# Attention projection: the parts of q and k stored once, and stacks put together by the loads

## The chip, the cores and the metric

One NeuronCore of a Trainium2 chip runs the whole program in one launch. Its engines are TensorE (PE, with its weight loads as PEld), VectorE (DVE), ScalarE (ACT), GpSimd (POOL) and SyncE (SP); 16 DMA engines move data, on one queue that SyncE issues to and one that ScalarE issues to. The metric is the device time of one execution in microseconds. Three executions of the kernel before took 5768.95, 5780.09 and 5784.97 us, the median is 5780.09 us.

## The reference, cut to what matters

The program is a stack of sixteen layers on four sequences of 1024 tokens with 128 features. Five of the layers are attention (layers 2, 4, 6, 8 and 14 of the program). The others (state space layers, ternary and gated feed-forward layers, a mixture of experts) are not touched. An attention layer computes, with 16 heads of 8 features (layer 14: 4 features for q and k):

```
h = layernorm(x)
q, k, v = h @ Wq + bq, h @ Wk + bk, h @ Wv + bv      # split into 16 heads
q, k = rope(q), rope(k)                              # layers 4 and 6 alone
s = q k^T * scale, causal                            # layer 14 adds a slope times the distance
y = softmax(s) v                                     # layer 2 weighs the probabilities by a decay table
x = x + y @ Wo + bo
```

## The kernel before

The residual stream `x` stays in SBUF, features on partitions and 4096 tokens along them. Every layer is a chain of stages; a stage ends when all its engines have reached its end (a barrier), and the next then starts. `attention` (from line 419) has a layer norm, the projection `attn_project` and the core `attn_core`.

**The projection.** The 4096 tokens are worked through in four batches (the sequences), each as two halves of 512 tokens, q and k in turn: four units a batch. TensorE multiplies (L526), VectorE brings the value to SBUF, with a bias or with rotary embedding (L550 to L577), ScalarE rounds it to bf16 (L607, the high part), GpSimd subtracts (L643), ScalarE rounds the rest (L613, the middle part), and the low part is what is then left (L561 on VectorE, or L650 on GpSimd where there is rotary embedding). `part` holds the three bf16 parts of q and k. V is projected last (L532, L595, L598).

**Slots.** Scores are made with bf16 products whose sum comes close to a float32 product: six pairs of a part of q and a part of k, the list `PAIRS`. A head thus needs 6 x 8 rows of q (high, high, high, middle, middle, low) against 6 x 8 rows of k (high, middle, low, high, middle, high). The projection writes all six slots to DRAM: for each batch six DMAs for q, issued by SyncE (L511), and six for k, issued by ScalarE (`store_k`, L619). Each moves all heads of one slot, 128 partitions of 1024 tokens, 256 KB (128 KB in layer 14). `store_k(b - 1)` stands in ScalarE's program after the first activations of batch b.

**Stacks.** Four heads make a group, and there are 16 groups. A group's rows lie in SBUF as a stack, `qs[u]` and `ks[u]`: 64 partitions for each half of the heads (i), 2 x 1024 tokens along them (p). Three stacks are held at a time. `load_stack` (L443) loads one with four DMAs of 48 rows, each row two pieces of 2 KB, and two DMAs with zeros for the rows of the maxima (L445); layer 14 adds two more for its slopes (L449). The semaphore `stack_in[u]` counts them, and the core waits for `NST`. The first three stacks need batch 0 alone: SyncE issues them right behind batch 0's stores, once `first_stored` says that those have landed. At the stage's end SyncE waits until all stores have landed (`stored`).

**The core.** TensorE works through a written-out order (`PLAN`), in which each group has units a (scores for the maxima, L845, reduced by VectorE, L1019), units b (scores for the exponentials, L860, taken by ScalarE, L944) and values (L875). Units a run ahead by about one group: the first of group n + 2 come in the last third of the plan of group n. SyncE, in order: the maxima's rows of group n + 1 (L744, three DMAs of 8 KB into two partitions each); then, once all b of group n are done, the load of stack n + 3; then the group's sums (L750, L752). In some groups there are also DMAs of the sums of a whole batch (L759 to L769). L769 reads each of 16 (last batch: 12) rows of inverse sums eight times, for 128 (96) partitions.

Of the kernel before, what the change touches and what calls it, by code (L numbers as in the profile page):

```python
# [10 lines left out]
BF16 = mybir.dt.bfloat16  # L11
# [5 lines left out]
P = 128  # L17
B, S, D = 4, 1024, 128
T = B * S
NT = 512  # L20
# [377 lines left out]
HEADS = 16  # L398
# [2 lines left out]

PAIRS = ((0, 0), (0, 1), (0, 2), (1, 0), (1, 1), (2, 0))
AHEAD = 8


# [9 lines left out]
def attention(net, tag, w, dq, scale, rope=False, alibi=False, decay=False, bias=False, out_bias=False):  # L417

    nc = net.nc
    r0 = 6 * dq + (9 if alibi else 0)  # L420

    parts = {n: nc.dram_tensor(f"{tag}_{n}_rows", (B * HEADS * 6 * dq, S), BF16, kind="Internal").ap() for n in "qk"}
    heads_out = nc.dram_tensor(f"{tag}_heads_out", (B * P, S), F32, kind="Internal").ap()
    sums = nc.dram_tensor(f"{tag}_sums", (4 * GROUPS, S), F32, kind="Internal").ap()
    rsums = nc.dram_tensor(f"{tag}_rsums", (4 * GROUPS, S), F32, kind="Internal").ap()
    with stage(nc, tag) as (sb, ps, sem):
        v = sb("v", [P, GROUPS, KT, 4, 9])


        qs, ks = ([sb(f"{n}_rows_sb{u}", [P, 2, S], BF16) for u in range(3)] for n in "qk")  # L430
# [5 lines left out]
        c_in, stack_in = sem("consts_in"), [sem(f"stack_in{u}") for u in range(3)]  # L436

        def load_stack(sp, n):
            u = n % 3
            for n_, dst in (("q", qs[u]), ("k", ks[u])):  # L440
                src = parts[n_][n * 24 * dq:(n + 1) * 24 * dq, :].rearrange("(p i r) t -> i r p t", p=2, i=2)
                for i in range(2):
                    sp.dma_start(dst[64 * i:64 * i + 6 * dq, :, :], src[i]).then_inc(stack_in[u], 16)  # L443
            for i in range(2):
                sp.dma_start(qs[u][64 * i + r0:64 * i + r0 + 3, :, :],  # L445
                             net.dram["zero_rows"][:, 0:2, :]).then_inc(stack_in[u], 16)
                if alibi:
                    lines = net.dram["alibi_q"][n * 9:(n + 1) * 9].rearrange("r (p i) t -> i r p t", p=2)
                    sp.dma_start(qs[u][64 * i + 6 * dq:64 * i + r0, :, :], lines[i]).then_inc(stack_in[u], 16)  # L449
# [22 lines left out]
def attn_project(net, tag, w, dq, rope, bias, decay, parts, v, qs, ks, load_stack, load_consts_):  # L472


    nc, xn, dram = net.nc, net.xn, net.dram
    R = HEADS * dq
    with stage(nc, tag + "_proj") as (sb, ps, sem):
# [14 lines left out]
        part = sb("parts", [P, 2, 3, T], BF16)  # L492
# [7 lines left out]
        with nc.Block() as block:  # L500
            @block.sync
            def _(sp):

                sp.wait_ge(rows_clear, 6)
                load_consts_(sp)
                for b in range(B):
                    sp.wait_ge(hi, 4 * (b + 1))
                    sp.wait_ge(mid, 4 * (b + 1))
                    sp.wait_ge(low, 4 * (b + 1))
                    for slot in range(6):  # L510
                        sp.dma_start(parts["q"].rearrange("(b h s d) t -> b s h d t", b=B, s=6, d=dq)[b, slot],  # L511
                                     part[0:R, 0, PAIRS[slot][0], b * S:(b + 1) * S]
                                     ).then_inc(stored if b else first_stored, 16)
                    if b == 0:
                        sp.wait_ge(first_stored, 16 * 12)
                        for n in range(3):
                            load_stack(sp, n)
                sp.wait_ge(stored, 16 * 12 * (B - 1))
# [82 lines left out]
            @block.scalar  # L601
            def _(act):

                def first(b, m):
                    h, j = m // 2, m % 2
                    act.wait_ge(val, 4 * b + m + 1)
                    nc.scalar.activation(part[0:R, j, 0, ds(b * S + h * NT, NT)], t1[0:R, j, h, :],  # L607
                                         ACT.Copy).then_inc(hi, 1)

                def second(b, m):  # L610
                    h, j = m // 2, m % 2
                    act.wait_ge(rest, 4 * b + m + 1)
                    nc.scalar.activation(part[0:R, j, 1, ds(b * S + h * NT, NT)], t1[0:R, j, h, :],  # L613
                                         ACT.Copy).then_inc(mid, 1)

                def store_k(b):
                    act.wait_ge(low, 4 * b + 4)
                    for slot in range(6):
                        act.dma_start(parts["k"].rearrange("(b h s d) t -> b s h d t", b=B, s=6, d=dq)[b, slot],  # L619
                                      part[0:R, 1, PAIRS[slot][1], b * S:(b + 1) * S]  # L620
                                      ).then_inc(stored if b else first_stored, 16)

                for b in range(B):
                    for m in range(4):
                        first(b, m)
                        if m:
                            second(b, m - 1)
                        if b and m == 1:
                            store_k(b - 1)
                    second(b, 3)  # L630
                store_k(B - 1)

            @block.gpsimd
            def _(pool):
# [31 lines left out]
def attn_core(net, tag, w, dq, r0, scale, alibi, decay, out_bias, v, qs, ks, heads_out, sums, rsums, consts, c_in,  # L666
# [35 lines left out]
    with stage(nc, tag + "_core") as (sb, ps, sem):  # L702
# [26 lines left out]
        cut = sem("diagonal_cut")  # L729
        o_stored, dec_ready, z_ready = [sem(f"out_stored{u}") for u in range(2)], sem("decayed"), sem("acc_zeroed")  # L730

        NST = 16 * (6 + (2 if alibi else 0))
        WIN = 16 * (7 if out_bias else 6)
        CIN = 16 * (6 + 6 + (6 if alibi else 0) + (2 if decay else 0))
        MIN = 16 * 3
# [1801 lines left out]
    return np.stack([hi, mid, low])  # L2537


def shape_constants():  # L2540

    bf = mybir.dt.np(BF16)
# [2 lines left out]

    d = np.arange(P) % 8
    freq = (1.0 / 10000.0 ** ((d // 2 * 2).astype(f) / 8)).astype(f)
    theta = pos[None] * freq[:, None]
    sign = np.where(d % 2 == 0, -1.0, 1.0).astype(f)[:, None]
    rope = np.stack([np.cos(theta), np.sin(theta) * sign], 1).astype(f)  # L2550

    i = np.arange(P)
# [36 lines left out]
def attention_layouts(i):  # L2589
    row, one = (lambda v: v.reshape(1, -1)), (lambda v: v.reshape(-1, 1))  # L2590
    swap = np.arange(P) ^ 1
    out = {}
    w = i["L0_attn_b_W_attn"]
    out.update(a0_wq=w[:, :P], a0_wk=w[:, P:2 * P], a0_wv=w[:, 2 * P:], a0_wo=i["L0_attn_b_W_proj"])
    for n, wn, f in (("a1", "L1_attn_a_w", lambda m: m.T), ("b1", "L1_attn_b_W", lambda m: m)):
        q, k, bq, bk = f(i[wn + "q"]), f(i[wn + "k"]), i[wn[:-1] + "bq"], i[wn[:-1] + "bk"]
        out.update({f"{n}_wq": q, f"{n}_wk": k, f"{n}_wv": f(i[wn + "v"]), f"{n}_wo": f(i[wn + "o"]),
                    f"{n}_wq_sw": q[:, swap], f"{n}_wk_sw": k[:, swap], f"{n}_bq": one(bq), f"{n}_bk": one(bk),
                    f"{n}_bq_sw": one(bq[swap]), f"{n}_bk_sw": one(bk[swap]),
                    f"{n}_bv": row(i[wn[:-1] + "bv"]), f"{n}_bo": one(i[wn[:-1] + "bo"])})  # L2600
    w = i["L2_attn_a_attn_W"].reshape(D, HEADS, 3, 8)
    b = i["L2_attn_a_attn_b"].reshape(HEADS, 3, 8)
    for j, n in enumerate("qkv"):
        out[f"a2_w{n}"] = w[:, :, j].reshape(D, P)
        out[f"a2_b{n}"] = (row if n == "v" else one)(b[:, j].reshape(P))
    out.update(a2_wo=i["L2_attn_a_out_W"], a2_bo=one(i["L2_attn_a_out_b"]))
    out.update(b3_wq=np.tile(i["L3_attn_b_Wq"], (1, 2)), b3_wk=np.tile(i["L3_attn_b_Wk"], (1, 8)),
               b3_wv=np.tile(i["L3_attn_b_Wv"], (1, 4)), b3_wo=i["L3_attn_b_Wp"], b3_bo=one(i["L3_attn_b_bp"]))
    return out

# [100 lines left out]
```

## Time and profile before

| | us |
|---|---|
| median of three executions | 5780.09 |
| the profiled execution | 5786.37 |
| its span, first to last instruction | 5784.7 |
| projection of the second attention, first matmul at | 1590.55 |
| first matmul of its core (L845) at | 1670.58 |
| second attention, first exponential at | 1700.72 |

Times in the rows are microseconds from the start of the profiled span. "PEclk" is the granted share of TensorE's full clock of 2.4 GHz. "x6" says that a row has merged six instructions. A number in brackets behind a row of a timeline is the idle time of the engine ahead of it and what ended that.

### The profile page before, as it was taken

Reading aid. Unit: us, or ns where it says so; the run is one execution under the profiler, and the core shown is the slowest. Engines: PE = TensorE matmul, PEld = TensorE weight load, DVE = VectorE, ACT = ScalarE, POOL = GpSimd, SP = SyncE. Lnnn points to the kernel's source line nnn. Section 1 sums busy time; section 2 is a strip of 40 time slices with the busy share of each in tenths; the row PEclk is TensorE's granted clock in tenths of the full one; section 3 lists DMA queues with packets and bytes.
Section 4 is the critical chain, followed back from the end, with each engine's and each line's share of the span. In section 5 each row is a group of like instructions: output and inputs, shape, how many; then the busy total and the mean of one; then the engine's idle time right before and its main releaser. Section 6 shows DMA issues by size and latency. Waiting matters only on the chain. (4 is left out here: it accounts for less than half of the span.)

```text
span 5784.7 us, 90553 instructions
## 1 busy us (share of the span) xinstructions
PE 4739.9 (82%) x33501; PEld 2093.1 (36%) x33596; DVE 3851.3 (67%) x4812; ACT 3154.0 (55%) x6002; POOL 1570.5 (27%) x1188
## 2 busy tenths in 40 slices
PE   5677667998569977699777998589877799699999
PEld 2233223443223336233353333256432344233344
DVE  6899658886579953799537993577638710699510
ACT  5665444766438853388534885444466521388621
POOL 0666315886032215322152220000006400122100
PEclk7899888999779989799897999789989999799999
DMA  0000012111031225322253220000000000211100
GB/s 27 0 1 1 4 54 71 44 44 29 10 114 43 53 60 181 114 50 51 62 166 120 50 46 20 6 10 2 5 10 0 20 0 0 59 31 45 42 0 15
DMA packets 146883, 239.82 MB, mean 41 GB/s; under 512 B 37382, under 2 KB 66930, under 8 KB 145076
## 3 DMA queue, kind: packets, MB, share of 16 engines
q1 hardware_dynamic: 125748, 197.74, 12.9%
q10 hardware_dynamic: 15744, 28.32, 1.5%
q0 software_dynamic: 4992, 8.41, 0.6%
q8 instruction: 254, 4.16, 0.3%
q14 instruction: 145, 1.19, 0.1%
HBM read 153.93 MB, written 80.31 MB: 40 GB/s over the span
## 5 line engine op out<-in xcount | busy, mean ns | idle before, releaser
L944 ACT ACTIVATE l_core_probs<-l_core_ps_scores_b 128x512 f32<-128x512 f32 (+3 forms) x3840 | 1599.6, 506 | 590.8 <-PE l_core_ps_scores_b L860 432.5
L1019 DVE TENSOR_REDUCE l_core_chunk_max<-l_core_ps_scores_a 128x2 f32<-128x1024 f32 (+3 forms) x1280 | 1237.1, 1020 | 86.7 <-PE l_core_ps_scores_a L845 51.9
L860 PE MATMUL l_core_ps_scores_b<-l_q_rows_sb,l_k_rows_sb 64*128 64x512 bf16 (+3 forms) x3840 | 908.8, 332 | 22.2 <-ACT l_core_probs L944 9.6
L845 PE MATMUL l_core_ps_scores_a<-l_k_rows_sb,l_q_rows_sb 64*128 64x512 bf16 (+3 forms) x3840 | 802.1, 344 | 116.4 <-DVE l_core_chunk_max L1019 53.4
L972 POOL TENSOR_SCALAR_AFFINE_SELECT l_core_probs<-l_core_probs 128x512 f32<-128x512 f32 x512 | 331.2, 647 | 1451.5 <-ACT l_core_probs L944 1451.5
L875 PE MATMUL l_core_ps_acc<-l_core_probs,l_v 128*9 128x512 f32 (+3 forms) x6144 | 644.3, 491 | 12.4 <-ACT l_core_probs L944 1.9
L1019 DVE TENSOR_REDUCE l_core_neg_max<-l_core_ps_scores_a 128x2 f32<-128x256 f32 (+3 forms) x640 | 499.0, 818 | 50.0 <-PE l_core_ps_scores_a L805 34.0
L860 PEld LDWEIGHTS l_core_ps_scores_b<-l_q_rows_sb,l_k_rows_sb 64*128 64x128 bf16 x3840 | 282.7, 93 | 652.8 <-ACT l_core_probs L944 552.8
L1882 POOL TENSOR_TENSOR l_scan_bx<-l_xs,l_scan_b_rows 128x1024 f32<-128x1024 f32 x192 | 452.0, 2355 | 225.0 <-DVE l_scan_states L1892 217.0
L1892 DVE TENSOR_TENSOR_SCAN l_scan_states<-l_scan_ps_decay,l_scan_bx 128x1024 f32<-128x1024 f32 x192 | 439.8, 2290 | 40.6 <-POOL l_scan_bx L1882 15.3
L963 POOL TENSOR_TENSOR l_core_probs_decayed<-l_core_probs,l_decay 128x1536 f32<-128x1536 f32 (+2 forms) x160 | 394.0, 2487 | 142.2 <-ACT l_core_probs L944 142.2
L805 PE MATMUL l_core_ps_scores_a<-l_mask_q_rows,l_identity_halves 64*128 64x64 bf16 (+1 forms) x5120 | 418.6, 211 | 0.0
L1827 PE MATMUL l_scan_ps_y<-l_scan_states_c,ident 128*128 128x512 f32 x768 | 363.2, 596 | 0.0
L805 PEld LDWEIGHTS l_core_ps_scores_a<-l_mask_q_rows,l_identity_halves 64*128 64x128 bf16 x5120 | 325.2, 98 | 93.1 <-issue 13.5
L845 PEld LDWEIGHTS l_core_ps_scores_a<-l_k_rows_sb,l_q_rows_sb 64*128 64x128 bf16 x3840 | 212.4, 94 | 388.8 <-DVE l_core_chunk_max L1019 228.1
L1855 ACT ACTIVATE l_scan_ps_decay<-l_delta,l_a_cols 128x1024 f32<-128x1024 f32 x192 | 214.6, 1118 | 251.6 <-DVE l_scan_states L1892 251.6
L1526 DVE SCALAR_TENSOR_TENSOR x_res<-l_ps_out,l_scales,x_res 128x512 f32 x16 | 12.0, 751 | 487.0 <-PE l_ps_out L1499 487.0
L1515 ACT ACTIVATE l_gelu<-l_ps_hidden,l_scales 128x512 f32<-128x512 f32 x128 | 87.9, 687 | 384.8 <-PE l_ps_hidden L1487 384.8
L1777 POOL TENSOR_TENSOR l_xs<-l_xs,l_delta x16 | 28.9, 1805 | 776.5 <-DVE l_delta L1767 776.5
L1817 PE MATMUL l_scan_ps_c_rows<-l_bc_parts,l_spread 128*128 128x512 bf16 x371 | 115.4, 390 | 150.2 <-DVE l_scan_states_c L1900 150.2
L1900 DVE TENSOR_TENSOR l_scan_states_c<-l_scan_states,l_scan_ps_c_rows 128x1024 f32<-128x1024 f32 x192 | 229.6, 1196 | 1.8 <-PE l_scan_ps_c_rows L1817 1.8
L2299 ACT ACTIVATE x_norm<-l_chunks_ps_decay 128x1024 f32<-128x1024 f32 x128 | 131.1, 1024 | 179.6 <-PE l_chunks_ps_decay L2243 179.6
(317 smaller groups left out, 7513.0 us busy)
## 6 DMA issues: line engine op xcount, KB each, us to landing
l_slots_weights<-m_both_dram SPq DMA_DIRECT2D x78, 512.0 KB, 4.8
l_k_rows<-l_proj_parts ACTq DMA_DIRECT2D x96, 256.0 KB, 5.5
l_q_rows<-l_proj_parts SPq DMA_DIRECT2D x96, 256.0 KB, 5.2
l_q_rows_sb<-l_q_rows SPq DMA_DIRECT2D x128, 192.0 KB
l_k_rows_sb<-l_k_rows SPq DMA_DIRECT2D x128, 192.0 KB
l_heads_out<-l_core_out_sums SPq DMA_DIRECT2D x300, 32.0 KB
l_core_heads<-l_heads_out SPq DMA_DIRECT2D x15, 512.0 KB, 4.1
l_core_inverse_rows<-l_rsums SPq DMA_DIRECT2D x15, 512.0 KB, 6.0
```

Of the source, the lines that this page charges most:

```text
L805: mm = nc.tensor.matmul(dst[:, cols[h]], eye[rows, h, :], mask[rows, h, cols[h]], start=False, stop=(h == 1))
L845: mm = nc.tensor.matmul(slot[:, i, 0:w], qs[n % 3][rows, p, qt * P:(qt + 1) * P], ks[n % 3][rows, p, c * NT:c * NT + w], start=True, stop= ...
L860: mm = nc.tensor.matmul(pb[m % 3][:, 0:w], ks[n % 3][rows, p, kt * P:(kt + 1) * P], qs[n % 3][rows, p, q0:q0 + w], start=True, stop=not diag)
L875: mm = nc.tensor.matmul(acc[32 * j:32 * j + 9, NT - w:NT], ones9[:, :] if decay else v[:, n, kt, j, :], pt[:, ts % RP, j, 0:w], start=(kt ...
L944: nc.scalar.activation(pt[:, ts % RP, j, 0:w], pb[m % 3][:, 0:w], ACT.Exp, scale=scale).then_inc(b_free, 1)
L963: nc.gpsimd.tensor_tensor(pw[:, had_decay(ts) % RW, :, 0:wd], pt[:, ts % RP, :, 0:wd], dtab[:, :, off:off + wd].to_broadcast((P, 4, wd)), ...
L972: nc.gpsimd.affine_select(block_, block_, [[0, 4], [1, P]], ALU.is_ge, none, base=0, channel_multiplier=-1).then_inc(cut, 1)
L1019: nc.vector.tensor_reduce(to, pa[e % 2][:, :, 0:width_a(qt, c)], AX.X, ALU.max, negate=True).then_inc(a_free, 1)
L1827: mm = nc.tensor.matmul(acc[:, c * NT:(c + 1) * NT], net.ident[:, :], hc[:, q % R, c * NT:(c + 1) * NT], start=(n == 0), stop=(n == NS - 1))
L1882: nc.gpsimd.tensor_tensor(bx[:, q % R, :], xs[:, h, b * S:(b + 1) * S], bs[:, q % RS, :], ALU.mult).then_inc(bx_done, 1)
L1892: nc.vector.tensor_tensor_scan(hs[:, q % RS, :], pa[:, :], bx[:, q % R, :], 0.0, ALU.mult, ALU.add).then_inc(scanned, 1)
L1900: nc.vector.tensor_tensor(hc[:, q % R, :], hs[:, q % RS, :], pc[:, :], ALU.mult).then_inc(hc_done, 1)
```

## The change

Each of the three parts of q and k is now stored once. `parts` is a DRAM tensor of three planes. SyncE issues all stores, after each half batch: three for q and three for k, each 128 partitions of 512 tokens (1 KB), 128 KB; `store_k` on ScalarE is gone. The stack is put together by the loads. `RUNS` lists runs of slots which share one part of q: slots 0 to 2 (the high part), 3 and 4 (the middle part), 5 (the low part). In each run the source of q is that part, repeated as many times as the run has slots, and the source of k is the first parts of the three planes, as many. So a stack takes twelve DMAs of rows of 4 KB and two of zeros. The load of the first three stacks moves from behind batch 0's stores to behind batch 2's. Within the columns of each four heads, q and k columns are reordered on the host (by half i, then feature, then p), so that the rows of p = 0 and p = 1 lie next to each other in DRAM; weights, biases and the rotary table are permuted to fit.

```diff
-PAIRS = ((0, 0), (0, 1), (0, 2), (1, 0), (1, 1), (2, 0))
+RUNS = ((0, 0, 0, 3), (3, 1, 0, 2), (5, 2, 0, 1))
@@ attention
-    parts = {n: nc.dram_tensor(f"{tag}_{n}_rows", (B * HEADS * 6 * dq, S), BF16, kind="Internal").ap() for n in "qk"}
+    parts = {n: nc.dram_tensor(f"{tag}_{n}_rows", (3, B * HEADS * dq, S), BF16, kind="Internal").ap() for n in "qk"}
@@ load_stack
-            for n_, dst in (("q", qs[u]), ("k", ks[u])):
-                src = parts[n_][n * 24 * dq:(n + 1) * 24 * dq, :].rearrange("(p i r) t -> i r p t", p=2, i=2)
-                for i in range(2):
-                    sp.dma_start(dst[64 * i:64 * i + 6 * dq, :, :], src[i]).then_inc(stack_in[u], 16)
+            for i in range(2):
+                lines = slice(n * 4 * dq + i * 2 * dq, n * 4 * dq + (i + 1) * 2 * dq)
+                for at, part, first, slots in RUNS:
+                    rows = slice(64 * i + at * dq, 64 * i + (at + slots) * dq)
+                    src = parts["q"][part, lines, :].rearrange("(o d p) t -> o d (p t)", o=1, p=2)
+                    sp.dma_start(qs[u][rows, :, :].rearrange("r p t -> r (p t)"),
+                                 src.to_broadcast((slots, dq, 2 * S))).then_inc(stack_in[u], 16)
+                    src = parts["k"][first:first + slots, lines, :].rearrange("s (d p) t -> s d (p t)", p=2)
+                    sp.dma_start(ks[u][rows, :, :].rearrange("r p t -> r (p t)"), src).then_inc(stack_in[u], 16)
@@ attn_project, SyncE
                 for b in range(B):
-                    sp.wait_ge(hi, 4 * (b + 1))
-                    sp.wait_ge(mid, 4 * (b + 1))
-                    sp.wait_ge(low, 4 * (b + 1))
-                    for slot in range(6):
-                        sp.dma_start(parts["q"].rearrange("(b h s d) t -> b s h d t", b=B, s=6, d=dq)[b, slot],
-                                     part[0:R, 0, PAIRS[slot][0], b * S:(b + 1) * S]
-                                     ).then_inc(stored if b else first_stored, 16)
-                    if b == 0:
+                    for h in range(2):
+                        sp.wait_ge(hi, 4 * b + 2 * h + 2)
+                        sp.wait_ge(mid, 4 * b + 2 * h + 2)
+                        sp.wait_ge(low, 4 * b + 2 * h + 2)
+                        for j, n in enumerate("qk"):
+                            for s_ in range(3):
+                                sp.dma_start(parts[n][s_, b * R:(b + 1) * R, h * NT:(h + 1) * NT],
+                                             part[0:R, j, s_, b * S + h * NT:b * S + (h + 1) * NT]
+                                             ).then_inc(stored if b else first_stored, 16)
+                    if b == 2:
                         sp.wait_ge(first_stored, 16 * 12)
                         for n in range(3):
                             load_stack(sp, n)
@@ attn_project, ScalarE
-                def store_k(b):
-                    act.wait_ge(low, 4 * b + 4)
-                    for slot in range(6):
-                        act.dma_start(parts["k"].rearrange("(b h s d) t -> b s h d t", b=B, s=6, d=dq)[b, slot],
-                                      part[0:R, 1, PAIRS[slot][1], b * S:(b + 1) * S]
-                                      ).then_inc(stored if b else first_stored, 16)
-
                 for b in range(B):
                     for m in range(4):
                         first(b, m)
                         if m:
                             second(b, m - 1)
-                        if b and m == 1:
-                            store_k(b - 1)
                     second(b, 3)
-                store_k(B - 1)
@@ attn_core
-        NST = 16 * (6 + (2 if alibi else 0))
+        NST = 16 * (14 + (2 if alibi else 0))
@@ host
+def stack_order(dq):
+
+    return np.arange(HEADS * dq).reshape(4, 2, 2, dq).transpose(0, 2, 3, 1).reshape(-1)
```

## Rows read from the trace of the kernel before

**Rows 1.** The page: the span, and the busy time of each engine.
```profile
span 5784.7 us, 90553 instructions
PE 4739.9 (82%) x33501; PEld 2093.1 (36%) x33596; DVE 3851.3 (67%) x4812; ACT 3154.0 (55%) x6002; POOL 1570.5 (27%) x1188
```

**Rows 2.** Busy time by stretch, second attention: stretch, length, engines, clock, DMA share, GB/s.
```profile
1630.00:1645.00 15.00, 10.62 (x33) 5.22 (x32) 11.96 (x14) 4.76 (x9) 11.57 (x10) 0.93 1.05 335
1655.00:1670.00 15.00, 0.00 (x0) 0.00 (x0) 0.01 (x1) 0.39 (x2) 1.80 (x2) 0.54 0.65 210
1670.00:1700.00 30.00, 18.71 (x159) 7.68 (x161) 27.72 (x38) 1.09 (x1) 0.00 (x0) 0.50 0.01 2
```

**Rows 3.** Timeline of ScalarE's queue, second attention: start, us, engine, line, operation.
```profile
1612.90 7.46 ACTq L619 DMA_DIRECT2D l_k_rows<-l_proj_parts  x6
```

**Rows 4.** Timeline of GpSimd, second attention, batch 0.
```profile
1603.88 1.15 POOL L643 TENSOR_TENSOR l_proj_t<-l_proj_t,l_proj_parts 128x512 f32<-128x512 f32 x1 [0.33 <-ACT l_proj_parts L613]
...
1606.93 1.16 POOL L643 TENSOR_TENSOR l_proj_t<-l_proj_t,l_proj_parts 128x512 f32<-128x512 f32 x1 [0.33 <-ACT l_proj_parts L613]
```

**Rows 5.** Timeline of VectorE, first attention, batch 0.
```profile
837.58 0.69 DVE L561 TENSOR_TENSOR l_proj_parts<-l_proj_t,l_proj_parts 128x512 bf16<-128x512 f32 x1
...
841.73 0.69 DVE L561 TENSOR_TENSOR l_proj_parts<-l_proj_t,l_proj_parts 128x512 bf16<-128x512 f32 x1 [0.15 <-DVE l_proj_t L553]
```

**Rows 6.** Timeline of SyncE: batch 0's q stores in attentions 1, 2, 4, 5.
```profile
842.53 6.47 SPq L511 DMA_DIRECT2D l_q_rows<-l_proj_parts  x6
...
1611.21 5.90 SPq L511 DMA_DIRECT2D l_q_rows<-l_proj_parts  x6
...
3040.75 0.58 SPq L511 DMA_DIRECT2D l_q_rows<-l_proj_parts  x1
...
4961.98 6.09 SPq L511 DMA_DIRECT2D l_q_rows<-l_proj_parts  x6
```

**Rows 7.** Timelines: the core's first matmuls in attentions 1, 2, 5; the fifth's last copy.
```profile
893.26 0.39 PE L805 MATMUL l_core_ps_scores_a<-l_mask_q_rows,l_identity_halves 64*128 64x128 bf16 x4
...
1670.58 0.29 PE L845 MATMUL l_core_ps_scores_a<-l_k_rows_sb,l_q_rows_sb 64*128 64x128 bf16 x2 [16.90 <-DVE l_core_ps_acc L977]
...
5004.12 0.89 DVE L598 COPY l_v<-l_proj_ps_v 128x128 f32<-128x128 f32 x4 [0.25 <-PE l_proj_ps_v L532]
...
5006.72 0.24 PE L845 MATMUL l_core_ps_scores_a<-l_k_rows_sb,l_q_rows_sb 64*128 64x128 bf16 x2
```

**Rows 8.** Busy by stretch: stores; heads; inverse rows; masks L454; maxima L744; last inverse rows.
```profile
868.00:881.00 13.00, 2.50 (x12) 2.20 (x11) 5.38 (x9) 3.21 (x6) 3.88 (x3) 0.63 1.00 357
1371.40:1373.00 1.60, 1.60 (x5) 0.53 (x3) 1.60 (x2) 0.49 (x1) 1.55 (x1) 0.55 0.84 333
1373.00:1374.50 1.50, 1.50 (x19) 0.41 (x20) 1.50 (x3) 0.00 (x0) 0.00 (x0) 1.00 0.87 243
...
1598.95:1599.15 0.20, 0.20 (x2) 0.00 (x0) 0.17 (x1) 0.00 (x0) 0.20 (x1) 1.00 0.53 120
1749.26:1749.44 0.18, 0.18 (x5) 0.11 (x4) 0.05 (x2) 0.18 (x2) 0.00 (x0) 1.00 0.16 37
...
2812.60:2813.50 0.90, 0.89 (x11) 0.21 (x9) 0.00 (x0) 0.83 (x2) 0.00 (x0) 1.00 0.69 246
```

**Rows 9.** Timelines of SyncE and TensorE in the second attention's core.
```profile
1748.09 1.59 SPq L744 DMA_DIRECT2D l_q_rows_sb<-l_core_max_parts  x3
1752.61 0.80 SPq L443 DMA_DIRECT2D l_q_rows_sb<-l_q_rows  x2
...
1755.56 0.62 SPq L445 DMA_DIRECT2D l_q_rows_sb<-zero_rows_dram  x2
...
1770.04 0.22 PE L845 MATMUL l_core_ps_scores_a<-l_k_rows_sb,l_q_rows_sb 64*128 64x128 bf16 x2
...
1772.70 1.59 SPq L744 DMA_DIRECT2D l_q_rows_sb<-l_core_max_parts  x3
```

**Rows 10.** Timeline of SyncE: a load of alibi rows in the fifth attention.
```profile
4974.32 0.83 SPq L449 DMA_DIRECT2D l_q_rows_sb<-alibi_q_dram  x1
```

More of the change, by code:

```diff
@@ L2547, in shape_constants @@
     freq = (1.0 / 10000.0 ** ((d // 2 * 2).astype(f) / 8)).astype(f)
-    theta = pos[None] * freq[:, None]
-    sign = np.where(d % 2 == 0, -1.0, 1.0).astype(f)[:, None]
+    order = stack_order(8)
+    theta = pos[None] * freq[order, None]
+    sign = np.where(d[order] % 2 == 0, -1.0, 1.0).astype(f)[:, None]
     rope = np.stack([np.cos(theta), np.sin(theta) * sign], 1).astype(f)
@@ L2591, in attention_layouts @@
     swap = np.arange(P) ^ 1
+    order, order4 = stack_order(8), np.tile(stack_order(4), 2)
     out = {}
     w = i["L0_attn_b_W_attn"]
-    out.update(a0_wq=w[:, :P], a0_wk=w[:, P:2 * P], a0_wv=w[:, 2 * P:], a0_wo=i["L0_attn_b_W_proj"])
+    out.update(a0_wq=w[:, :P][:, order], a0_wk=w[:, P:2 * P][:, order], a0_wv=w[:, 2 * P:], a0_wo=i["L0_attn_b_W_proj"])
     for n, wn, f in (("a1", "L1_attn_a_w", lambda m: m.T), ("b1", "L1_attn_b_W", lambda m: m)):
         q, k, bq, bk = f(i[wn + "q"]), f(i[wn + "k"]), i[wn[:-1] + "bq"], i[wn[:-1] + "bk"]
-        out.update({f"{n}_wq": q, f"{n}_wk": k, f"{n}_wv": f(i[wn + "v"]), f"{n}_wo": f(i[wn + "o"]),
-                    f"{n}_wq_sw": q[:, swap], f"{n}_wk_sw": k[:, swap], f"{n}_bq": one(bq), f"{n}_bk": one(bk),
-                    f"{n}_bq_sw": one(bq[swap]), f"{n}_bk_sw": one(bk[swap]),
+        out.update({f"{n}_wq": q[:, order], f"{n}_wk": k[:, order], f"{n}_wv": f(i[wn + "v"]), f"{n}_wo": f(i[wn + "o"]),
+                    f"{n}_wq_sw": q[:, swap[order]], f"{n}_wk_sw": k[:, swap[order]],
+                    f"{n}_bq": one(bq[order]), f"{n}_bk": one(bk[order]),
+                    f"{n}_bq_sw": one(bq[swap[order]]), f"{n}_bk_sw": one(bk[swap[order]]),
                     f"{n}_bv": row(i[wn[:-1] + "bv"]), f"{n}_bo": one(i[wn[:-1] + "bo"])})
@@ L2603, in attention_layouts @@
     for j, n in enumerate("qkv"):
-        out[f"a2_w{n}"] = w[:, :, j].reshape(D, P)
-        out[f"a2_b{n}"] = (row if n == "v" else one)(b[:, j].reshape(P))
+        cols = slice(None) if n == "v" else order
+        out[f"a2_w{n}"] = w[:, :, j].reshape(D, P)[:, cols]
+        out[f"a2_b{n}"] = (row if n == "v" else one)(b[:, j].reshape(P)[cols])
     out.update(a2_wo=i["L2_attn_a_out_W"], a2_bo=one(i["L2_attn_a_out_b"]))
-    out.update(b3_wq=np.tile(i["L3_attn_b_Wq"], (1, 2)), b3_wk=np.tile(i["L3_attn_b_Wk"], (1, 8)),
+    out.update(b3_wq=i["L3_attn_b_Wq"][:, order4], b3_wk=np.tile(i["L3_attn_b_Wk"], (1, 8))[:, order4],
                b3_wv=np.tile(i["L3_attn_b_Wv"], (1, 4)), b3_wo=i["L3_attn_b_Wp"], b3_bo=one(i["L3_attn_b_bp"]))
```

## The prediction

> **What bounds the kernel now.** I read the page first, then busy time by stretch, then the timelines of SyncE, ScalarE and TensorE around the five attention layers. The page [rows 1] shows a span of 5784.7 us with TensorE busy 82% of it; but the change touches only the attention layers, and there two stages have different limits. In the stretches of the second attention's projection [rows 2] the DMA engines are full (1.05 of their time at 335 GB/s) while TensorE, VectorE, ScalarE and GpSimd all have gaps; then 15 us follow in which no engine computes at all and only the last stores move (share 0.65), because the stage ends on the wait for `stored`. The 30 us behind it are the first group's maxima, bound by VectorE (27.7 of 30 us) at a granted clock of 0.50, that is 1.2 GHz; that is so before and will stay so. So projection is bound by stores, and its cost is seen as the time until the core's first matmul.
>
> **Part 1: k stores leave ScalarE, and stored bytes halve.** Each batch of the second attention costs ScalarE one block of six store issues, 7.46 us for the first [rows 3], and its activations stand still behind it. Without that block a batch runs at its own pace. That pace is in batch 0, ahead of any store: GpSimd starts one L643 every 3.05 us with rotary embedding [rows 4], and VectorE's L561 runs twice in 4.15 us without it, 2.08 us each [rows 5]. A batch is four of these: 12.2 us or 8.3 us. Batches 1 and 2 therefore end 24.4 us (16.6 us) behind batch 0, whose end is the first q store [rows 6]: 842.5, 1611.2, 3040.8 and 4962.0 us. In the sum this is the whole gain of the moved stores: what comes before the end of batch 2 ends earlier than it did. The stores are 12 a batch before and after (6 for each half now), but 128 KB each. SyncE issues all of them; one that meets no backlog takes 0.58 us to issue (3040.75 [rows 6]), so six cost 3.5 us, less than the 4.2 us in which a half batch is made.
>
> **Part 2: the first three stacks are loaded two batches later.** Before, they go out behind batch 0. Now SyncE issues them behind batch 2's stores and ahead of batch 3's. All that is issued: 3 x (12 loads + 2 zero rows) = 42 DMAs. Behind them in the same queue stand batch 3's 12 stores, for which the stage's end waits. So whatever the loads take beyond the 8.3 or 12.2 us of batch 3 is bare. The first three matmuls of the core that I compare with start at 893.3, 1670.6 and 5006.7 us [rows 7].
>
> **Part 3: loads with an outermost dimension of 3, 2 and 1.** A half stack was one DMA of 48 rows by 2 x 2 KB for q and one for k. It is now three for each, with (slots, dq) rows of 4 KB: 3 x 8, 2 x 8 and 1 x 8. How widely does such a DMA spread? Rows 8 have both kinds at the same packet size (256 B): the mask loads with 64 rows outermost use 0.53 of the DMA engines at 120 GB/s; the maxima's rows, 8 KB each with 2 outermost and 16 pieces behind, use 0.16 at 37 GB/s, some 2 of 16 engines, though there are 32 pieces to share out. And the inverse rows of the last batch, 96 rows at the destination but 12 heads outermost at the source, use 0.69, under 12/16 = 0.75, where the stores with 16 outermost reach 1.00. I read from this that a DMA runs on as many engines as its outermost dimension allows: 3, 2 and 8 here. No row says whether two such DMAs take the same engines. I take the same ones, since nothing in a DMA's description would tell them apart; the other end is an even spread (a rival below).
>
> The Trainium skill ("DMA: Bandwidth & Descriptors", section "Why a DMA increments its semaphore by 16 and not by 1") states both: the count is the largest number up to 16 that divides the outermost sizes of both sides, and from SyncE they are the lowest-numbered ones. The rows agree with the first part (0.16 and 0.69); no row here can show the second. By that rule the sum would be the one below; without it, the rival's.
>
> The price of a 4 KB piece on one engine: the saturated stretch moves 357 GB/s at share 1.00, which is 22.3 GB/s an engine or 0.184 us; loads of whole rows 333 GB/s at 0.84, or 0.165 us; the broadcast inverse rows 243 at 0.87, or 0.235 us [rows 8]. I take 0.17: next to the 0.165 of plain loads, as the other engines lie idle; the q loads are broadcasts, so 0.235 stays an upper end. Pieces of a stack on the busiest engine: 24/3 + 16/2 + 8/8 = 17 for q and for k, in two halves: 68, and 2 zero rows: 70, or 11.9 us. Three stacks: 35.7 us (34.7 to 49.4). The queue in front of an engine is short (six stores of 256 KB already hold SyncE for 5.9 to 6.5 us [rows 6]), so SyncE is held back too.
>
> **The sum at the start.** From the end of batch 2: six stores issued 3.5, first packet 1.0 (estimate; the maxima's rows issued at 1748.09 [rows 9] move at 1749.26 [rows 8]), loads 35.7, batch 3's stores on the busiest engine 12 x 8 x 1 KB at 0.046 = 4.4, landing 0.5 (estimate), and from the last work of a stage to the first matmul 1.7 (5005.01 to 5006.72 [rows 7]): 46.8 us. First attention: 842.5 + 16.6 + 46.8 = 905.9 against 893.3, +12.6. Second: 1611.2 + 24.4 + 46.8 = 1682.4 against 1670.6, +11.8. The third repeats the second and the fourth the first: +11.8, +12.6. The fifth has half the pieces, and SyncE's issue is what lasts: 14 DMAs at 0.35 (0.31 [rows 9] and a gap) and 2 alibi rows at 0.88 [rows 10] are 6.7 us a stack, 20.0 for three; 12 stores 7.0; 1.5 to land; 1.7: 4962.0 + 16.6 + 3.5 + 30.2 = 5012.3 against 5006.7, +5.6. Together +54 us.
>
> **The sum in the core: 0, with a thin cover.** A stack for group n + 3 is issued when group n's exponentials have their scores, 1752.61, and first read at 1770.04 [rows 9]: 17.4 us. With 16 engines a stack's 768 KB needed few of them; now it needs 70 x 0.17 + 1.7 (first packet, landing) = 13.6 us. The same engines then carry the eight small stores of the heads' sums, which nobody waits for within the group, and the maxima's rows, issued 20 us behind the load (1772.70; a group is 24.6 us, from 1748.09) and so behind its end. Slack left: 3.8 us. It is gone at 0.224 us a piece. Fourteen issues at 0.35 are 4.9 us of SyncE, well inside a group. Laying q and k columns out by stack only permutes weights, biases and table rows ahead of the launch: 0.
>
> The profiled execution took 5786.4 us (span 5784.7, 1.7 around it), the median of three runs is 5780.1. Forecast: 5840 profiled, 5834 on the scale of the median.
>
> **Rivals.**
> *Even spread (ends on the other side).* If narrow DMAs take different engines, no engine carries more than about 2.3 MB / 16 and SyncE's issue decides: 42 x 0.35 = 14.7 in place of 35.7, then 12 stores 7.0, 1.5, 1.7 and the first 3.5: 28.4 us. First attention 887.5 (-5.8), second 1664.0 (-6.6), again twice, fifth +5.6: -19 us, 5761, and some 10 us less if stores issue faster than 0.58. Against it: 0.16 and 37 GB/s show the narrowness, and only the choice of engines is open. It decides from the point where busiest-engine work falls below 25 us.
> *Thin cover torn.* If a piece costs 0.235 us in k as in q, a stack lands after 70 x 0.235 + 1.7 = 18.2 us, 0.8 us late, in 13 groups of the three attentions with 25 us groups: 31 us; the start grows by 210 x 0.065 = 13.7 in four: 55 us. 5920. For it: the broadcast row. Against: there 12 engines work at once, here 3.
> *Gain and loss cancel.* If SyncE is not held back and batch 3's stores pass on the thirteen or so other engines while only the lowest lag, and pieces run at the 0.165 end, part of the tail hides; with a faster batch pace the net could be within 17 us: 5785.
> That the change doesn't do what it says can be left out: the stored bytes follow from the shapes.
>
> **How the numbers follow.** Forecast 65%, its own range 5812 (pieces at 0.165, batches at their pace, less 20) to 5870 (q at 0.235: +27, stalls of a few us); even spread 16%, torn cover 8%, cancelled 11%. Changes under 0.3% (17 us) can't be told from none. Faster: most of the even spread, 0.14. Same: the rest of it and the cancelled case, 0.15. Slower 0.71. The range 5762 to 5900 leaves out most of the even spread and the worst of the torn cover.
>
> **What would show it.** Right: no DMA issue on ScalarE; activations at 3.05 us steps through all batches; from the end of batch 2 a stretch of some 35 us with a DMA share near 0.15 to 0.25 and SyncE held in the loads; first matmuls of the core near 906 and 1682. In the core the group stays 24.6 us and no wait for a load shows ahead of the scores. Wrong: a DMA share near 0.5 during the loads and a projection that ends before 893 or 1670; or idle TensorE time ended by a load in every group.

## The result, and the profile after

The changed kernel takes 5882.13 us (median of 4 runs, 5868.99 to 5885.52), against 5780.66 for the kernel before in the same session (4 runs, 5768.95 to 5784.97): a ratio of 1.0168, 95% interval 1.0153 to 1.0183. The forecast was 5834, in a range of 5762 to 5900, with slower at 0.71. So the direction held, and half of the loss was missing: 5882 lies above the forecast's own 5812 to 5870, and inside the stated range only because the rivals had widened it. The profiled execution took 5878.81 us, its span is 92.4 us longer than in [rows 1]:

```profile
span 5877.1 us, 91308 instructions
PE 4749.2 (81%) x33596; PEld 2088.1 (36%) x33596; DVE 3846.1 (65%) x4812; ACT 3154.4 (54%) x6002; POOL 1572.6 (27%) x1188
...
HBM read 153.93 MB, written 52.00 MB: 35 GB/s over the span
```

Busy times are what they were; the time is all in waits. The stores did shrink: 52.00 MB are written, and before it was

```profile
HBM read 153.93 MB, written 80.31 MB: 40 GB/s over the span
```

To find the waits I cut each attention in two: from the projection's first matmul to the core's first (the start, which [rows 7] ends), and from there through the last of units b (the core; the 29.2 to 29.5 us from first a to first b change nowhere and are left out). Worked out from TensorE's timeline, in us, for attentions 1 to 5:

```
                  start                            core (first b to last b)
before    67.8   80.0   80.2   68.1   61.5     487.7  400.9  402.1  401.1  400.9
after     78.2   90.0   90.0   77.6   76.8     489.6  416.1  413.8  413.2  399.6
change   +10.4  +10.0   +9.8   +9.5  +15.3      +1.9  +15.2  +11.7  +12.1   -1.3
```

The starts lose 55 us, as forecast (54). The cores lose 40, where the forecast had 0.

**The start.** Busy time by stretch in the first attention, after (stretch, length, five engines, clock, DMA share, GB/s): batches 1 and 2; the loads, which SyncE issues from 861.87; batch 3's stores; and the end.

```profile
843.00:859.00 16.00, 12.10 (x32) 4.73 (x32) 13.69 (x18) 10.29 (x18) 10.44 (x10) 0.89 0.61 213
862.00:887.00 25.00, 8.05 (x48) 7.55 (x48) 8.36 (x34) 0.63 (x1) 0.24 (x1) 0.64 0.24 82
887.00:898.00 11.00, 0.00 (x0) 0.00 (x0) 0.00 (x0) 0.00 (x0) 0.00 (x0) 0.50 0.44 157
898.00:903.00 5.00, 0.00 (x0) 0.00 (x0) 0.00 (x0) 0.00 (x0) 0.00 (x0) 0.50 0.26 89
```

The DMA engines are no longer full in the batches (0.61; 1.00 in [rows 8]). Then for 25 us the loads run at a share of 0.24 and 82 GB/s, as if on four engines of 16. The stores behind them lift the share only to 0.44, and the last 5 us are back at 0.26. That last row mixes two things. After 899.3 only two engines still move data:

```profile
899.40:903.20 3.80, 0.00 (x0) 0.00 (x0) 0.00 (x0) 0.00 (x0) 0.00 (x0) 0.50 0.12 43
```

0.12 of 16 is two engines, and 43 GB/s over two is 22 each, the rate of a busy engine in [rows 8]. The semaphore `stored` tells the same: each of batch 3's twelve stores adds 16 to it in steps of one. Of these 192 steps, 168 have come by 899.30; the last 24, two a store, follow one by one, every 0.17 us, until 903.27. Everybody waits for the two engines that carry both the loads and their share of the stores. SyncE's timeline has the order (start, us, engine, line, operation):

```profile
866.44 0.70 SPq L451 DMA_DIRECT2D l_k_rows_sb<-l_k_rows  x1
867.18 0.63 SPq L448 DMA_DIRECT2D l_q_rows_sb<-l_q_rows  x1
...
868.51 0.48 SPq L448 DMA_DIRECT2D l_q_rows_sb<-l_q_rows  x1
869.03 0.29 SPq L451 DMA_DIRECT2D l_k_rows_sb<-l_k_rows  x1
...
886.30 0.59 SPq L453 DMA_DIRECT2D l_q_rows_sb<-zero_rows_dram  x2
887.01 2.80 SPq L521 DMA_DIRECT2D l_q_rows<-l_proj_parts  x3
889.85 3.11 SPq L521 DMA_DIRECT2D l_k_rows<-l_proj_parts  x3
893.07 3.35 SPq L521 DMA_DIRECT2D l_q_rows<-l_proj_parts  x3
```

Batch 3's stores take about 1 us each to issue. The core's first matmuls, the answer to [rows 7], with the idle time before them in brackets:

```profile
904.95 0.29 PE L845 MATMUL l_core_ps_scores_a<-l_k_rows_sb,l_q_rows_sb 64*128 64x128 bf16 x2 [32.43 <-DVE l_core_ps_acc L977]
...
1694.33 0.29 PE L845 MATMUL l_core_ps_scores_a<-l_k_rows_sb,l_q_rows_sb 64*128 64x128 bf16 x2 [30.03 <-DVE l_core_ps_acc L977]
...
5097.72 0.29 PE L845 MATMUL l_core_ps_scores_a<-l_k_rows_sb,l_q_rows_sb 64*128 64x128 bf16 x2 [31.05 <-DVE l_core_ps_acc L977]
```

The profile puts this idle time down to VectorE, which had long been done; no engine computes in the last 17 us, and the windows show what runs. The releaser named in a row is only the best guess among several semaphores.

**The core.** In attentions 2 to 4 a group still lasts 24.5 us, but three groups in each last 28.7 to 30.5 us instead of 24.9: those in which the sums of a whole batch come back. VectorE's waits, second attention's core of after (us in total, times, longest):

```profile
DVE l_core_inverse L982 <- DMA l_core_inverse<-l_sums: 12.5, 4, 3.8
```

The last of the four, 3.8 us at the core's end, is there before as well (4.3). The other three are new: 8.7 us of VectorE. Here is how the first arises. Timelines of SyncE and VectorE, before:

```profile
1826.25 0.80 SPq L443 DMA_DIRECT2D l_q_rows_sb<-l_q_rows  x2
...
1828.76 0.35 SPq L759 DMA_DIRECT2D l_core_inverse<-l_sums  x1
...
1838.55 0.94 DVE L982 RECIPROCAL l_core_inverse<-l_core_inverse 128x128 f32<-128x128 f32 x1
```

And after:

```profile
1848.82 0.72 SPq L448 DMA_DIRECT2D l_q_rows_sb<-l_q_rows  x1
...
1856.12 0.60 SPq L453 DMA_DIRECT2D l_q_rows_sb<-zero_rows_dram  x2
1856.83 0.36 SPq L759 DMA_DIRECT2D l_core_inverse<-l_sums  x1
...
1863.64 0.95 DVE L982 RECIPROCAL l_core_inverse<-l_core_inverse 128x128 f32<-128x128 f32 x1 [2.45 <-DMA l_core_inverse<-l_sums]
```

From the lists of DMA issues (count, KB each, median us from issue to landing), before:

```profile
l_core_inverse<-l_sums SPq DMA_DIRECT2D x15, 64.0 KB, 3.6
```

and after:

```profile
l_core_inverse<-l_sums SPq DMA_DIRECT2D x15, 64.0 KB, 6.9
```

Before, the read of the sums stands 2.5 us behind the start of the stack's load, lands 3.6 us later (1832.3), and VectorE takes it at 1838.55: 6.2 us of slack. After, it stands 8.0 us behind, since fourteen issues replace six, and lands 6.8 us after its issue, since it queues behind the narrow loads: 14 of the 16 steps of its semaphore come 1.6 to 2.3 us after the issue, the last two at 6.2 and 6.8. So again two engines of 16 are behind. 5.5 + 3.2 = 8.7 us later, 2.5 more than the slack. The row shows 2.45. While VectorE waits it takes no maxima:

```profile
1865.74 0.61 PE L845 MATMUL l_core_ps_scores_a<-l_k_rows_sb,l_q_rows_sb 64*128 64x512 bf16 x2 [2.74 <-DVE l_core_chunk_max L1019]
```

Attention 1 has longer groups (30.1 us) and so more slack, attention 5 half the rows: neither stalls.

### The profile page after: what moved, and what is told of

Its sections match the earlier page's. It is cut to its first block and busy times, and to the rows that moved or that the text cites. A ratio compares the mean times of both kernels' runs of the same rounds, so it can differ in the third digit from the quotient of the medians.

```text
span 5877.1 us, 91308 instructions
## 1 busy us (share of the span) xinstructions
PE 4749.2 (81%) x33596; PEld 2088.1 (36%) x33596; DVE 3846.1 (65%) x4812; ACT 3154.4 (54%) x6002; POOL 1572.6 (27%) x1188
## 5 line engine op out<-in xcount | busy, mean ns | idle before, releaser
L1892 DVE TENSOR_TENSOR_SCAN l_scan_states<-l_scan_ps_decay,l_scan_bx 128x1024 f32<-128x1024 f32 x192 | 439.7, 2290 | 40.8 <-POOL l_scan_bx L1882 15.3
```

The lines of the kernel that those rows point to most:

```text
L1892: nc.vector.tensor_tensor_scan(hs[:, q % RS, :], pa[:, :], bx[:, q % R, :], 0.0, ALU.mult, ALU.add).then_inc(scanned, 1)
```

## The experiments

They ran on two other chips, on which the kernel before takes 5811.97 us (23 runs) and 5812.36 us (7 runs); so ratios compare, not microseconds, and 1% is 58 us. The first four runs shared one chip, the last four the other. "The start" and "the core" are the columns above.

**wide8: the same loads, spread over more engines.** The changed kernel, but with the feature as the outermost dimension of each load; rows and bytes are the same.

```
-    src = parts["q"][part, lines, :].rearrange("(o d p) t -> o d (p t)", o=1, p=2)
-    ... src.to_broadcast((slots, dq, 2 * S))
-    src = parts["k"][first:first + slots, lines, :].rearrange("s (d p) t -> s d (p t)", p=2)
+    src = parts["q"][part, lines, :].rearrange("(o d p) t -> d o (p t)", o=1, p=2)
+    ... src.to_broadcast((dq, slots, 2 * S))
+    src = parts["k"][first:first + slots, lines, :].rearrange("s (d p) t -> d s (p t)", p=2)
```

> The changed kernel with one edit: in the loads of a stack the feature is the outermost dimension and the slot the next (rows in the order feature, slot for q and k alike), so all twelve DMAs have 8 outermost (4 in layer 14) in place of 3, 2 and 8. Bytes, pieces of 4 KB, number of DMAs and their place are unchanged. Theory A (a narrow DMA runs on the same few DMA engines each time, and what queues behind it waits): the busiest engine has 26 pieces a stack in place of 70, so batch 3's stores are no longer blocked and the start of each core comes about 9 us earlier in the first four attentions (first about 896 in place of 905), 2 us in the fifth, and VectorE's waits for the sums in groups 4, 8 and 12 go (about 40 us in all): 5805 us. Theory B (SyncE's issue time of 25 us for 42 DMAs is what costs, engines do not matter): nothing changes, 5882 us. Theory C (q's repeated reading of one source is slow): unchanged, 5882 us.

Measured: 1.0028 (1.0018 to 1.0039) of before. The starts are 68.0, 80.3, 80.4, 68.5 and 75.9 us, the cores 489.4, 402.8, 401.6, 403.1 and 401.4. In the first four attentions both losses are gone; the fifth keeps its own. The loads, and batch 3's stores behind them:

```profile
862.00:887.00 25.00, 8.06 (x48) 7.68 (x48) 8.55 (x34) 0.63 (x1) 0.42 (x1) 0.64 0.36 109
887.00:893.00 6.00, 0.00 (x0) 0.00 (x0) 0.00 (x0) 0.00 (x0) 0.00 (x0) 0.50 0.74 257
```

SyncE in the same stretch:

```profile
867.25 0.65 SPq L448 DMA_DIRECT2D l_q_rows_sb<-l_q_rows  x1
...
887.39 1.46 SPq L521 DMA_DIRECT2D l_k_rows<-l_proj_parts  x3
```

The issue of a load costs what it did (0.65 us), and 25 us for three stacks remain; but the stores now pass at a share of 0.74, and three of them issue in 1.46 instead of 3.11 us. So it is the width, not the count of DMAs, that costs the four starts 10 us each, and that tips the sums over in the core. There the first read of the sums is issued as late as in the change, 8.1 us behind the start of the load, but lands 2.1 us after its issue in place of 6.8:

```profile
DVE l_core_inverse L982 <- DMA l_core_inverse<-l_sums: 3.7, 1, 3.7
```

The semaphore of a stack shows the width itself. Each load of a stack adds 72 steps in the change and 116 in wide8. Read as one step for each engine of a DMA, the 44 more are what twelve DMAs on 8 engines (96) have over four on 3, four on 2 and four on 8 (52).

**sums_first: only the order in the core.** The changed kernel, with the batch's sums read (L759) ahead of the stack's load in the groups after 4, 8 and 12.

```
+                    if n >= 4 and n % 4 == 0:
+                        sums_back(n // 4 - 1, HEADS)
                     ...   # load_stack(sp, n + 3), then the sums of the group
-                    if n >= 4 and n % 4 == 0:
-                        sums_back(n // 4 - 1, HEADS)
```

> The changed kernel with one edit: in SyncE's order within the core the DMA that brings the sums of a batch back (L759) is issued ahead of the load of a stack in groups 4, 8 and 12, in place of behind it. Theory A (the second half of the loss is VectorE's wait for these sums, which stand behind the loads in the queue): the 25 us groups keep their length everywhere, 40 us less than the changed kernel, the start of the cores unchanged: 5842 us. Rival D (the groups are longer since the stacks themselves, or the maxima's rows, come late): no change, 5882 us.

Measured: 1.0100 (1.0083 to 1.0117), against 1.0168 for the change: 40 us less. The starts are as in the change (78.2, 90.1, 90.7, 77.8, 76.8), the cores 489.6, 400.6, 402.1, 400.9 and 399.4. The loads are as narrow and as slow to issue as before, and the wait is gone:

```profile
DVE l_core_inverse L982 <- DMA l_core_inverse<-l_sums: 4.0, 1, 4.0
```

That settles the core: the 40 us are the place of one 64 KB read in SyncE's queue. Taken with wide8, neither the longer issue alone nor the place alone is too much; issue and backlog together are.

**narrow_before: inconclusive.** The kernel before, with its loads written as three slots outermost.

```
-    src = parts[n_][...].rearrange("(p i r) t -> i r p t", p=2, i=2)
+    src = parts[n_][...].rearrange("(p i s r) t -> i s r p t", p=2, i=2, s=3)
```

> The kernel before with one edit: the source of each load of a stack has its 48 rows as 3 x 16 (3 outermost), so that each of the same four DMAs a stack of 192 KB should run on 3 DMA engines in place of 16. Six slots are still stored, number and place of DMAs unchanged. Theory A: 256 KB a stack on each of three engines, some 11 us in place of under 3. The first three stacks (33 us) are loaded behind batch 0 and stores queue behind them: the starts of the first four cores come later by some 5 to 15 us each; SyncE issues few DMAs, so the sums are issued early (2.5 us behind the group's end) but land behind the load at about 14 us, 2 us later than VectorE asks: waits of about 2 us in groups 4, 8 and 12 of three attentions, 15 us. In all 5780 + 30 to 75. Theory B (issue time and number of DMAs cost, engines do not matter): 5780 us.

Measured: 0.9998 (0.9989 to 1.0008), nothing moved. It isolates nothing: s and r lie one behind the other in memory, so three slots of 16 rows are the same 48 rows, and during a load the DMA share in the core is 0.64 (0.63 in the kernel before), not a quarter of the engines. A load adds 72 steps to its semaphore in both, where four DMAs on 3 engines in place of 16 would add 52 fewer.

```profile
1751.00:1756.00 5.00, 4.93 (x59) 2.10 (x56) 4.68 (x6) 4.89 (x14) 1.90 (x3) 1.00 0.64 161
```

A form that keeps the three apart in the kernel before wasn't tried.

**k_on_sp: the issues off ScalarE, without halving the bytes.** The kernel before, with SyncE issuing the k stores.

```
+    for j, n in enumerate("qk"):
         for slot in range(6):
-            sp.dma_start(parts["q"]...[b, slot], part[0:R, 0, PAIRS[slot][0], ...])
+            sp.dma_start(parts[n]...[b, slot], part[0:R, j, PAIRS[slot][j], ...])
...
-                        if b and m == 1:
-                            store_k(b - 1)
...
-                store_k(B - 1)
```

> The kernel before with one edit: SyncE issues the k stores too, behind the q stores of each batch; ScalarE issues none. Six slots of 256 KB are still stored. Theory A (before, the projection is bound by the DMA engines, which are full from batch 0 on, and ScalarE's blocks only follow from that): the batches are made earlier but the last store lands as late, so the start of the cores moves by less than 3 us each, 5780 within 10. Rival E (ScalarE's blocks of 4 to 7 us are themselves what makes the batches late): 5 to 10 us less in each of five attentions, 5740.

Measured: 0.9982 (0.9973 to 0.9992). The starts are 67.5, 70.4, 71.9, 67.0 and 65.8: the two attentions with rotary embedding gain 8 to 10 us, the two plain ones of 8 features nothing, the fifth loses 4 (why wasn't followed). So neither expectation holds as put: A fails with rotary embedding, E without. The second attention's stretch from the first store to the last, k_on_sp:

```profile
1614.00:1659.00 45.00, 27.23 (x100) 15.08 (x100) 33.11 (x63) 13.66 (x23) 30.85 (x24) 0.92 0.98 319
```

and the same in the kernel before:

```profile
1611.00:1668.50 57.50, 27.96 (x100) 14.69 (x100) 33.33 (x63) 13.61 (x23) 29.32 (x25) 0.83 0.84 261
```

With rotary embedding ScalarE's six issues of 7.46 us [rows 3] did hold the batches up, and without them the same bytes pass at a share of 0.98. At that point the DMA engines are full, and the plain attentions, whose batches are shorter, are near it already: in the kernel before the first attention's stores run at a share of 0.94 (845 to 891). What can still be gained there has to come from fewer bytes or from another place of the loads.

**late_before: only the later loads.** The kernel before (wide loads), with the first three stacks behind batch 2.

```
-                    if b == 0:
+                    if b == 2:
```

> The kernel before with one edit: the first three stacks are loaded behind batch 2's stores in place of batch 0's. Its loads have 48 rows outermost and take 16 DMA engines. Theory A (place alone costs nothing where the loads are wide and few, as the DMA engines are full throughout and their total is unchanged): starts within 5 us of before, ratio 1.000 within 0.003. Theory H (the later place is what cost the changed kernel its start): 10 us more in each attention, ratio 1.008.

Measured: 1.0052 (1.0036 to 1.0069); the starts grow by 4.8, 5.3, 4.1, 6.6 and 6.9 us, 28 in all. The later place costs half of what the starts of the changed kernel lose, and that with stores twice as large as the changed kernel's; it ended between the sizes expected.

**loads_b0: only the place undone.** The changed kernel with `if b == 0`.

> The changed kernel with one edit: the first three stacks are loaded behind batch 0's stores again, in place of batch 2's. The loads keep 3, 2 and 8 outermost. Theory A: the busiest engine's 36 us then lie beside batches 1 to 3, but all 36 stores behind them wait: batch 0's end + 2.8 + 2 + 35.7 + 36 x 8 x 0.046 = 13.3, + 2.2: start 73 us behind the first matmul without rotary embedding (78 changed), 77 with it (90), 72 in the fifth (77): 41 us less than the changed kernel, ratio 1.0097; the waits in groups 4, 8 and 12 stay. Theory H (the place is all of the start's loss): start as before or earlier, 68 and 80 or less. Theory B (issue time alone): 65 and 70.

Measured: 1.0094 (1.0077 to 1.0111). The starts are 72.2, 75.5, 75.7, 72.1 and 78.3: 39 us less than in the change, and as expected but for the fifth. The cores keep their waits (414.9, 412.2, 413.2). So place and width each undo about 40 us of the starts' loss: narrow loads hurt because the stage's last stores stand right behind them; issued early, they have three batches beside which to pass. In the fifth attention the place changes little: its price is SyncE's issue, in either place.

**placed_narrow and best: the loads out of the way.** The changed kernel with stack 0 alone behind batch 1's stores, and stacks 1 and 2 as the first that SyncE issues in the core. `placed_narrow` is that alone; `best` adds wide8's dimensions and sums_first's order.

```
-                    if b == 2:
+                    if b == 1:
                         sp.wait_ge(first_stored, 16 * 12)
-                        for n in range(3):
-                            load_stack(sp, n)
+                        load_stack(sp, 0)
...
+                load_stack(sp, 1)      # attn_core, SyncE, ahead of its first wait
+                load_stack(sp, 2)
```

> The changed kernel with one edit: stack 0 is loaded behind batch 1's stores, stacks 1 and 2 at the head of SyncE's work in the core; loads keep 3, 2 and 8 outermost and the sums stay behind them. Theory A: the narrow queue is out of the stage's tail, so the start gains some 25 us in each of four attentions and 25 in the fifth against the changed kernel; in the core two stacks take 24 us on the busiest engines, and the first group's maxima rows, asked for at about 25 us, may come a few us late; the waits of 4 us in groups 4, 8 and 12 stay (40 us). Ratio to before 1.0168 - 0.021 = 0.996 to 1.000. Theory G (narrowness alone matters, place does not): ratio 1.0168.

> The changed kernel with three edits: 8 outermost in all stack loads (4 in layer 14), the sums brought back ahead of the load, and the first three stacks placed apart: stack 0 behind batch 1's stores, stacks 1 and 2 at the head of SyncE's work in the core, where nothing waits for them for 24 us and more. Theory A (stores halved and off ScalarE leave a stage bound by its engines, once narrow queues and 25 us of issue are out of its tail): first core matmul 48 to 50 us behind the first projection matmul without rotary embedding (67.8 before) and 62 with it (80.0 before), 48 in the fifth (61.5 before), the cores as before: 85 us less than before, ratio 0.985. Rival F (halved stores bring nothing, since the core then waits for its stacks or for the maxima's rows behind them): ratio 1.00.

Measured: `placed_narrow` 0.9943 (0.9925 to 0.9961), `best` 0.9875 (0.9859 to 0.9892), 5738.56 us against 5812.36. The starts of `best` are 50.5, 62.5, 62.7, 50.5 and 56.4, 75 us under those of before, its cores 487.7, 401.4, 400.1, 401.1 and 401.3. In `placed_narrow` the starts are the same within 2 us, and the cores have the wait (418.4, 414.2, 415.0). The second attention's core begins in `best` at 1636.10, and the maxima of its first group, in a stretch that answers to the last of [rows 2], run while the two stacks arrive:

```profile
1630.00:1660.00 30.00, 18.07 (x151) 8.82 (x149) 26.35 (x46) 1.28 (x1) 0.00 (x0) 0.60 0.26 81
```

```profile
1636.10 0.29 PE L846 MATMUL l_core_ps_scores_a<-l_k_rows_sb,l_q_rows_sb 64*128 64x128 bf16 x2 [2.46 <-DVE l_core_ps_acc L978]
```

`best` takes 74 us off the kernel before, for 85 expected; most of what is missing is the fifth attention (56.4 for 48). The idle time before the core's first matmul is 2.46 us, in place of 16.9 before [rows 7] and 30.03 after. So with halved stores, none of them on ScalarE, and no load between the last ones and the core, the start is some 17 us shorter in each of four attentions and 5 in the fifth. How much of that is the halving isn't shown: no run moved the loads of the kernel before into the core, which would relieve its full DMA engines too.

## Why the prediction was right, and what it missed

**Batches at their own pace: right.** ScalarE issues nothing any more, and batch 2 ends 15.0 us (24.0 with rotary embedding) behind batch 0, for 16.6 (24.4) forecast. GpSimd steps at 3.05 us in batch 2 as well, where [rows 4] had batch 0:

```profile
1641.62 1.15 POOL L643 TENSOR_TENSOR l_proj_t<-l_proj_t,l_proj_parts 128x512 f32<-128x512 f32 x1 [0.33 <-ACT l_proj_parts L623]
...
1644.67 1.16 POOL L643 TENSOR_TENSOR l_proj_t<-l_proj_t,l_proj_parts 128x512 f32<-128x512 f32 x1 [0.33 <-ACT l_proj_parts L623]
```

k_on_sp, which moved the issues and left the bytes, gained nothing in the plain attentions: taking the issues off ScalarE doesn't shorten a start whose DMA engines are full.

**The busiest engine decides behind the loads: right.** From the first load's issue, 861.87, the forecast's terms give 1.0 + 35.7 + 4.4 + 0.5 + 1.7 = 43.3, 905.2; the first matmul came at 904.95. wide8 takes the narrowness away and the loss goes. That rules out the even spread and the cancelled case: what the stage waited for is 17 pieces of 4 KB for each half of q and of k, 210 in three stacks with the zero rows, one after the other at 0.17 us. No trace here names the engines that carry a narrow DMA. That the DMAs of 3 and of 2 outermost share two of them, the point that the forecast had to assume, shows in the 0.12 at the end and in the two late steps of `stored` and of the sums' semaphore. One sign didn't come as put: SyncE was not held for 35 us. The loads' issue took 25.0 us at its own price, and only its last DMAs and the stores behind (1 us each) were held back.

The Trainium skill ("DMA: Bandwidth & Descriptors", section "Rules for kernel authors") says that a small outermost dimension, a leading broadcast with stride zero included, confines the DMA to at most that many engines. The runs agree: a share of 0.24 with 3, 2 and 8 outermost, 0.36 with 8 (4 in the fifth attention) at an unchanged rate of issue, and 1.4% of the time between the two kernels.

**The fifth attention: term mis-sized.** The step failed that said "14 DMAs at 0.35 (0.31 [rows 9] and a gap)". The fifth start took 15.3 us more, for 5.6 forecast. Its loads' issue runs from 5056.90 to 5086.67, 29.8 us for 20.0 forecast, since a load of the new shape costs SyncE 0.70, 0.63, 0.43 or 0.29 us. The 0.31 was the price of a zero row; the old loads in the same rows cost 0.40. In the other four the same issue (25.0 us) hid beside the busiest engine's 35.7. They lost 39.7 us for 48.8 forecast, about 2 us each, mostly because the plain batches were quicker and the loads began earlier. So the 55 us met the 54 partly by two errors of 9 to 10 us that cancel.

**The core at nothing: failed.** The step as put: "the eight small stores of the heads' sums, which nobody waits for within the group". It listed what stands behind the load in SyncE's queue and left out the one DMA of the list that VectorE waits for in the same group, L759. What I did work out held nearly: a stack has landed 14.7 us after its first issue in 42 of the 52 groups of the first four attentions (14.4 to 14.9), for 13.6 forecast and 17.4 allowed. In the other ten it takes 15.2 to 17.7, and TensorE waits for it once, for 0.36 us:

```profile
1919.93 0.23 PE L845 MATMUL l_core_ps_scores_a<-l_k_rows_sb,l_q_rows_sb 64*128 64x128 bf16 x2 [0.36 <-DMA l_q_rows_sb<-zero_rows_dram]
```

So the cover was as thin as forecast. But a queue that becomes 5.5 us longer must be followed to all that stand in it. The 6.2 us of slack was in the trace of before (1832.3 to 1838.55) and wasn't read. The torn cover, priced at 31 us in the core and 55 at the start, was the nearest rival in size, by another mechanism: the load's own landing, which was late that once.

How 2.5 us of VectorE's wait become 3.8 us of a group (28.7 for 24.9 from one issue of the maxima's rows to the next) is not settled: TensorE's own wait for the maxima is 2.74 us, and the rest wasn't followed. That sums_first returns all of it shows that it hangs on the same wait.

**Balance.** Over the five attentions against the kernel before, in us: the change +95 (55 + 40); width undone +21; place undone +54; order in the core undone +56; place mended further, narrow -28; all three -76.

## What to carry to other kernels

Write a DMA so that its outermost dimension is large, and judge a load by the pieces on its busiest engine, not by its bytes; a narrow one costs little by itself and much ahead of stores on which a stage's end waits. When a queue's work grows, list every DMA behind it and who waits for each, with the slack of each read from the trace, the small ones above all. Halving a transfer need not pay while something else stands between its last part and those who wait: here kernels with the same halved stores took 1.7% more or 1.2% less than the kernel before, by the place, shape and order of the loads.

## What the runs showed of the hardware beyond that

- The issue of a DMA on SyncE depends on its shape at equal row size: 0.70 us for 24 rows of 4 KB, 0.63 for 16, 0.43 for 8 of q and 0.29 for 8 of k, in the second core, where little else moves (1849.58 to 1855.78), as at the stage's end, and nearly unchanged by the order of the dimensions (0.66, 0.65, 0.46, 0.29 in wide8). The old loads, 48 rows of two 2 KB pieces, cost 0.40 to 0.45.
- A 64 KB read issued right behind a stack's load landed 6.9 us after its issue (median) behind the narrow loads, at a DMA share of only 0.23 (1849.00 to 1863.60), 3.6 behind the four wide DMAs of the kernel before, and 1.8 to 2.1 in the second core of wide8.
- 48 rows that lie one behind the other in memory and are written as 3 x 16 did not make a narrow DMA: 0.64 of the engines, 72 semaphore steps a stack as before, and 0.9998 of the time in narrow_before.
